# Slot expert outputs carried from SBUF to SBUF in eight small transfers per expert, instead of through DRAM

## The reference, cut to what matters

```python
logits = jnp.einsum('bmd,npd->bmnp', x, phi_n)                 # n = 64 experts, p = 16 slots
D = jax.nn.softmax(logits, axis=1)
C = jax.nn.softmax(logits.reshape(bsz, m, n * p), axis=-1)
Xs = jnp.einsum('bmd,bmnp->bnpd', x, D)
hdn = _layernorm(Xs, ln_g[:, None, :], ln_b[:, None, :])
hdn = jnp.einsum('bnpd,ndh->bnph', hdn, w1) + b1[:, None, :]
hdn = jax.nn.gelu(hdn, approximate=False)
Ys = jnp.einsum('bnph,nhd->bnpd', hdn, w2) + b2[:, None, :]
Y = jnp.einsum('bsd,bms->bmd', Ys.reshape(bsz, n * p, d), C)   # and the result is h + Y
```

## Time and profile before

| | us |
|---|---|
| median of 3 runs | 2728.07 (2725.43 to 2729.15) |
| the profiled execution, its own time | 2731.55 |
| its span | 2729.8 |
| `experts`, from the first store group on SP to the first load of `combine` | 192.1 (2457.7 to 2649.8) |
| `combine` to the end of the span | 80.0 (2649.8 to 2729.8) |

### The profile page before, as it was taken

How to read it: one execution, slowest core, us unless ns; L and a number is a source line. 1 busy time by engine, 2 the same in 40 slices (tenths; PEclk the granted TensorE clock), 3 DMA queues, 4 the chain that set the end, 5 groups by cost and what they waited for, 6 DMA issues and landing times. The chain is left out here.

```text
span 2729.8 us, 47824 instructions
## 1 busy us (share of the span) xinstructions
PE 2345.5 (86%) x16381; PEld 2105.8 (77%) x16381; DVE 1443.7 (53%) x3648; ACT 1260.3 (46%) x2142; POOL 870.8 (32%) x758
## 2 busy tenths in 40 slices
PE   1999999999999999999977656299697888868878
PEld 0899999999999999999977435288354566558778
DVE  6465565655556565565646785233575555532112
ACT  0667667676666767667653101011333544522220
POOL 3445455454545545454433231500330000000000
PEclk9999999999999999999988775699898988869989
DMA  1000000000000000000000004200100010117865
GB/s 52 3 4 2 4 2 4 2 2 4 2 4 2 2 4 2 4 2 4 2 3 1 0 0 135 73 14 18 26 14 4 34 46 35 46 58 248 265 202 205
DMA packets 66016, 104.89 MB, mean 38 GB/s; under 512 B 9589, under 2 KB 52255, under 8 KB 64861
## 3 DMA queue, kind: packets, MB, share of 16 engines
q1 hardware_dynamic: 51102, 80.77, 9.1%
q10 hardware_dynamic: 9280, 14.00, 1.5%
q0 software_dynamic: 5568, 9.27, 1.2%
HBM read 75.44 MB, written 28.49 MB: 38 GB/s over the span
## 5 line engine op out<-in xcount | busy, mean ns | idle before, releaser
L228 PE MATMUL bank<-t_wt,t_l 128*128 128x128 f32 x8508 | 1099.2, 283 | 4.1 <-ACT t_l L302 2.6
L228 PEld LDWEIGHTS bank<-t_wt,t_l 128*128 128x128 f32 x8508 | 1069.5, 198 | 16.9 <-ACT t_l L302 3.7
L398 POOL TENSOR_TENSOR t_rstd<-t_var,t_minus_half 128x4 f32<-128x4 f32 (+1 forms) x379 | 366.6, 967 | 693.1 <-DVE t_var L327 693.1
L315 ACT ACTIVATE t_l<-bank,t_cols 128x512 f32<-128x512 f32 x384 | 467.5, 1245 | 3.2 <-ACT t_l L310 0.3
L335 DVE TENSOR_TENSOR t_yn<-bank,t_rstd 128x512 f32<-128x512 f32 (+1 forms) x379 | 249.0, 657 | 333.5 <-POOL t_rstd L398 333.5
L285 ACT ACTIVATE t_sq<-bank 128x512 f32<-128x512 f32 (+1 forms) x379 | 217.7, 574 | 433.2 <-PE bank L228 433.2
L324 DVE TENSOR_REDUCE t_ss<-t_sq 128x4 f32<-128x512 f32 (+1 forms) x379 | 245.4, 647 | 177.3 <-ACT t_sq L285 177.3
L404 POOL TENSOR_TENSOR t_zrstd<-t_zvar,t_minus_half 128x8 f32<-128x8 f32 x196 | 320.7, 1637 | 43.0 <-DVE t_zvar L362 43.0
L302 ACT ACTIVATE t_l<-bank,t_cols 128x512 f32<-128x512 f32 (+2 forms) x381 | 282.5, 741 | 11.7 <-PE bank L237 6.9
L237 PE MATMUL bank<-t_ident,t_yn 128*128 128x128 f32 x1426 | 219.7, 274 | 11.4 <-DVE t_yn L335 10.1
L237 PEld LDWEIGHTS bank<-t_ident,t_yn 128*128 128x128 f32 x1426 | 172.0, 143 | 24.4 <-DVE t_yn L335 11.1
(11 more groups left out here) (317 smaller groups left out, 3493.7 us busy)
## 6 DMA issues: line engine op xcount, KB each, us to landing
t_w<-in_w SPq DMA_DIRECT2D x64, 480.0 KB
ect<-t_ECT SPq DMA_DIRECT2D x16, 750.0 KB, 3.2
t_ectb<-ect ACTq DMA_DIRECT2D x5, 1500.0 KB, 7.8
t_w1x<-in_w1x SPq DMA_DIRECT2D x64, 97.5 KB
ys<-t_ye SPq DMA_DIRECT2D x64, 96.0 KB
t_yb<-ys ACTq DMA_DIRECT2D x8, 768.0 KB, 10.8
t_ectb<-ect POOLq DMA_DIRECT2D x12, 375.0 KB, 6.1
t_xs<-in_x SPq DMA_DIRECT2D x50, 82.5 KB, 1.9
```

Source lines behind the costliest of these rows:

```text
L228: mm = pe.matmul(psY[bank][:, t * C:(t + 1) * C], src[:, at:at + 2 * P - 1:2], T["wt"][:, 3 * (layer - 1) + k, :], start=(k == 0), stop=(k ...
L315: act.activation(view(T["l0"][:, :], [[2, 4], [POS, P]], 2 + 8 * q + slot), psL[i % 2][:, :].rearrange("c (a p) -> c a p", a=4), ACT.Gelu, ...
L398: pool.tensor_tensor(T["rstd"][:, par, 0:n], T["var"][:, par, 0:n], T["minus_half"][:, 0:n], ALU.pow)\
```

## The change

Each expert's result no longer goes to `ys` in DRAM. `store` now issues eight DMAs per expert, one for each batch item: 16 partitions x 192 floats (12 KB) from `ye` to the place in `yb` where `combine` reads it. `yb` holds all eight items (48 KB in each partition instead of 18). `combine` has no `yb` loads any more, and the wait for `ectb` stands on PE instead of DVE. SP's loop over the experts is written out. To make room, `phA`/`phB` become one tensor `ph`, which is free by then and on which `ye`, `a1` and `a2` are laid, and `o` is laid on `eg`. The products, copies and biases are the same instructions on the same sizes.

```diff
             def store(sp, n, r):
                 sp.wait_ge(S["expert_read"], n + 3)
-                dst = bass.AP(io["ys"].tensor, n * SLOT * D, [[SLOTS * D, B], [D, SLOT], [1, D]])
-                sp.dma_start(dst, T["ye"][:, r, :]).then_inc(S[f"y_stored{r}"], 16)
-            with sp.Fori(0, SOFT_E - 2 * RING + 1, RING) as i:
-                for r in range(RING):
-                    sp.wait_ge(S["expert_out"], i + r + 1)
-                    load(sp, i + r + RING, r)
-                    store(sp, i + r, r)
+                at, c = n % (P // SLOT) * SLOT, n // (P // SLOT)
+                for b in range(B):
+                    sp.dma_start(T["yb"][at:at + SLOT, b, c, :], T["ye"][b * SLOT:(b + 1) * SLOT, r, :])\
+                        .then_inc(S[f"y_stored{r}"], 16)
+            for n in range(SOFT_E):
+                if n + RING < SOFT_E:
+                    sp.wait_ge(S["expert_out"], n + 1)
+                    load(sp, n + RING, n % RING)
+                store(sp, n, n % RING)
             for r in range(RING):
-                store(sp, SOFT_E - RING + r, r)
-            for r in range(RING):
-                sp.wait_ge(S[f"y_stored{r}"], 16 * SOFT_E // RING + 16)
+                sp.wait_ge(S[f"y_stored{r}"], 16 * B * (SOFT_E // RING + 1))
...
-                src = bass.AP(io["ys"].tensor, b * SLOTS * D, [[D, P], [P * D, SC], [1, D]])
-                act.dma_start(T["yb"][:, b % MIX_RING, :, :], src).then_inc(S[f"mix_loaded{b % MIX_RING}"], 16)
...
             def bias(b):
-                if b < MIX_RING:
-                    dve.wait_ge(S[f"mix_ahead{b}"], 16 * MIX_PIECES)
-                dve.wait_ge(S[f"mix_loaded{b % MIX_RING}"], 16 + 32 * (b // MIX_RING))
-                dve.tensor_tensor(T["yb"][:, b % MIX_RING, :, :], T["yb"][:, b % MIX_RING, :, :], T["b2s"][:, :, :], ALU.add)\
+                dve.tensor_tensor(T["yb"][:, b, :, :], T["yb"][:, b, :, :], T["b2s"][:, :, :], ALU.add)\
                     .then_inc(S["yb_ready"], 1)
...
             for b in range(B):
+                if b < MIX_RING:
+                    pe.wait_ge(S[f"mix_ahead{b}"], 16 * MIX_PIECES)
+                else:
+                    pe.wait_ge(S[f"mix_loaded{b % MIX_RING}"], 16 * (b // MIX_RING))
                 pe.wait_ge(S["yb_ready"], b + 1)
...
-            sx("yb", [P, MIX_RING, SC, D])
+            sx("yb", [P, B, SC, D])
```

More of the change, by code:

```diff
@@ L1875, in activations @@
                         gelu(i + r + 1, (r + 1) % RING)
-                    copy(i + r, r, 16 // RING * i + 16)
+                    copy(i + r, r, 16 * B // RING * i + 16 * B)
             gelu(0, 0)
@@ L1887, in _ @@
             for r in range(RING):
-                dve.sem_inc(S[f"y_stored{r}"], 16)
+                dve.sem_inc(S[f"y_stored{r}"], 16 * B)
             with dve.Fori(0, SOFT_E - RING + 1, RING) as i:
@@ L1957, in _ @@
                         mm = pe.matmul(pO[k % 2][0:n, 0:D], T["ectb"][:, b % MIX_RING, c, t * TOK:t * TOK + n],
-                                       T["yb"][:, b % MIX_RING, c, :], start=(c == 0), stop=(c == SC - 1))
+                                       T["yb"][:, b, c, :], start=(c == 0), stop=(c == SC - 1))
                     mm.then_inc(S["mixed"], 1)
@@ L2006, in program @@
         sb("h", [P, TILES, D])
-        sb("phA", [P, SLOTS])
-        sb("phB", [P, SLOTS])
+        sb("ph", [P, 2 * SLOTS])
+        T["phA"], T["phB"] = T["ph"][:, 0:SLOTS], T["ph"][:, SLOTS:2 * SLOTS]
         sb("egA", [P, 2, SOFT_E])
@@ L2184, in program @@
             sx("w1x", [D2 + 1, RING, SOFT_H])
-            sx("a1", [P, RING, P])
-            sx("a2", [D2 + 1, RING, P])
+            at = 0
+            for name, rows, n in (("ye", P, D), ("a1", P, P), ("a2", D2 + 1, P)):
+                T[name] = T["ph"][0:rows, at:at + RING * n].rearrange("p (r n) -> p r n", r=RING)
+                at += RING * n
             sx("eg", [P, 2, SOFT_H])
-            sx("ye", [P, RING, D])
             with nc.Block() as block:
@@ L2192, in _ @@
                     pool.memset(T["a2"][:, :, :], 1.0)
-            sx("yb", [P, MIX_RING, SC, D])
+            sx("yb", [P, B, SC, D])
             sx("ectb", [P, MIX_RING, SC, SEQ])
             experts(nc, T, S, io)
-            sx("o", [TOK, 4, D])
+            T["o"] = T["eg"][0:TOK, :, :].rearrange("p a (r n) -> p (a r) n", n=D)
             combine(nc, T, S, io)
```

## The result

| | before | changed |
|---|---|---|
| median, us | 2727.57 | 2914.88 (2913.88 to 2916.07) |
| ratio | | 1.0687, 95% interval 1.0669 to 1.0706 |
| span of the profiled execution, us | 2729.8 | 2913.4 |
| `experts` | 192.1 | 386.7 (2456.1 to 2842.8) |
| `combine` to the end of the span | 80.0 | 70.6 |

187 us slower, near the 2895 of the forecast and inside its range. `experts` took 194.6 us more, `combine` gave back 9.4, and the rest of the program was 1.6 us shorter in this execution (the stage began at 2456.1 instead of 2457.7).

The account below looks back on a forecast made before the run. PE and the weight loads pace `experts`; eight serial issues per expert would make SP the bound. `experts` +177.1 and `combine` -10.2 on 2731.55 give 2898 us profiled, 2895 for the median; range 2775 to 2985.

Parts of the forecast that it names:

- This is the number that the change has to live in: SP in `experts`: about 1.25 us to spare per expert, against the mean of 3.0 us.
- I = 0.62: SP in `experts`: time in us from one small-transfer issue to the next, midway between 0.76 and 0.48.
- By kind: SP's issue price in `experts`: nearest SBUF-to-SBUF row is L75, 0.706 us each, 0.76 from issue to issue.
- The loads, 0.83 for a pair: SP in `experts`: issuing an expert's two weight loads takes 0.83 us, counted 60 times.
- the 2898 of the sum: Whole kernel, profiled execution: 2731.55 + 177.1 - 10.2 = 2898 us.
- `combine`, -10.2: `combine`: 5.1 us gained without the first load and 5.1 without later waits, at most.
- Still hidden under 5.8: PE in `experts`: at its lower clock an expert takes 4.6 us, covered by SP's 5.8 us.
- PE idles more than half of the time: PE in `experts`: idle more than half of the time, so its clock may fall to the lower level.
- over 150 us: Sign in `experts`: PE's wait for the weight loads grows to over 150 us.
- So the loads meet no more traffic than before.: Weight loads in `experts`: as many 768-byte rows go to SBUF as went to DRAM, so no added cost.
- rival 2: SP in `experts`: issues below 0.27 us hide, only the gain of `combine` is left, kernel 2718 us; chance 0.04.
- The estimate of 0.43 us: SP's issue price in `experts`: 512 sequencer cycles at 1.2 GHz, putting the sum near 2823 us.

Follow-up runs that it names:

- the runs with four: Changed kernel with only the first four of the eight transfers per expert issued, the other outputs left out and `yb` zeroed beforehand: 2764.7 us.
- the spread kernel: Changed kernel with all eight transfers per expert, two issued on SP, two on ACT and four on POOL: 2738.7 us, ratio 1.0043 to the kernel before.
- the grouped kernel: Changed kernel with four experts' rows joined per SBUF-to-SBUF transfer, 128 instead of 512, issued by POOL: 2748.0 us, ratio 1.0070 to the kernel before.

## Why the prediction was right

- **The bound.** "This is the number that the change has to live in": about 1.25 us of spare time on SP for an expert, against eight issues of which the cheapest row took 0.25. This comparison decided the sign before the price was known, and the runs with four and with spread issues showed the bound moving as it says.
- **The price, I = 0.62.** Measured 0.62. The working reached it by the middle of two neighbours, and that was luck in part: the new transfer takes 0.59 + 0.04, the 10 x 10 form of L75 costs 0.71, and L1005 was cheaper since one end is in DRAM (0.42). "By kind" was the right neighbour, and its row had an extra that I couldn't see.
- **The loads, 0.83 for a pair.** Mis-sized: 1.08 in place of 0.83, 60 x 0.25 = 15 us. I took it from loads that follow loads; behind a copy inside SBUF the first of the pair takes 0.58. This one term is most of the 17 us by which the profiled execution (2915.2) missed the 2898 of the sum.
- **`combine`, -10.2.** Measured -9.4. No stall was left, as forecast; the first tile took 0.7 us more.
- **The cover.** "Still hidden under 5.8": PE's clock fell to 0.64 over the stage, and it cost nothing, as SP waited for PE for 8.1 us in all. But "PE idles more than half of the time" was wrong: at the lower clock its matmuls fill 70% of the stretch. So the sign "over 150 us" for PE's wait for the loads was missed too: it was 110.7.
- **"So the loads meet no more traffic than before."** True for bytes, wrong for the engines' time: 155 us in the changed kernel instead of 144. It cost nothing there, and came out where the issue was spread: the spread kernel is rival 2 in that its issue hides, and it was still 0.4% slower than before, with the DMA engines at 89% and 9.0 us more from the first copy to the last. My price of 2718 for that rival left this out. The rest of the difference is the late start of `combine`, which belongs to POOL's issues in that kernel and not to the rival.
- **The pages.** The estimate of 0.43 us from the Trainium skill ("DMA: Bandwidth & Descriptors", section "Why a DMA increments its semaphore by 16 and not by 1", with "Advanced Engine Details and Errata", section "Clock Domains") is near the transfers of 16 partitions with one end in DRAM (0.42), and not those of this change (0.59). The Trainium skill's remark that starting a DMA usually costs the sequencer little against the DMA itself ("DMA: Bandwidth & Descriptors", section "Issuing engines are not separate DMA queues") does not hold for these 12 KB: 0.62 us of SP each, one after the other, for transfers that land in 2.1 and overlap. The Trainium skill's rule to join small transfers (the same page, section "Rules for kernel authors") points the right way for the issue (512 to 128), but the grouped kernel shows that joining alone did not make them cheap for the engines.

## What to carry to other kernels

Before a transfer is cut in pieces, count the DMA instructions per step on the queue that also issues the loads, multiply by the issue time of a row of the same kind (both ends in SBUF, or one), and compare with the idle time of that queue per step: an issuing engine whose time stands in no busy column can be the bound. If the count is too high, spread the issues over the queues, and then look at the DMA engines' share, which is the next bound. A way through DRAM with one large store and large loads can be as good as the short way.

## What I had not expected of the hardware

- From SBUF to SBUF the issue on SP doesn't depend on size: 0.59 us for 768 bytes and 0.60 for 96 KB; 0.71 for 10 x 10. With one end in DRAM the same 16 partitions take 0.42.
- The price of a DMA depends on the one before it: `w12` takes 0.34 us behind another load (0.75 once, at the fourth pair), 0.42 behind a small store to DRAM, and 0.58 behind a copy inside SBUF. The copy itself takes 0.51 behind a load, as the first of the eight, and 0.59 behind another copy.
- POOL issues the same copy in 0.48 us, less than SP (0.59) or ACT (0.60).
- Where POOL issued DMAs up to the end of the stage, the engines' meeting behind it came 6.6 to 7.7 us late (0.2 in the other kernels).
- 6.3 MB between groups of 16 partitions keep the DMA engines busy for 30 to 57 us more, against 19 us to DRAM, and at full rate part of that is loads that take longer.
